# Block-quantised MLP on Trainium2: down projection as float32r products on halves, block maxima in a bank of the up projection

## The chip, the cores and the metric

The kernel runs on one core of a Trainium2 chip. The metric is device time in microseconds (us), the median of several executions. TensorE (PE) multiplies and transposes into the eight banks of PSUM; its weight loads are booked apart (PEld). VectorE (DVE) and ScalarE (ACT) read and write SBUF and the banks. GpSimd (POOL) works on SBUF here. SyncE (SP) starts the transfers.

## What is computed

Two decoder layers on `x` of 16 batches x 128 tokens x 256: attention, cross attention and an MLP each. The change is in the last MLP, which quantises every operand of its products in blocks of 32 columns:

```python
def _mx_dequant(t):
    rows, feat = t.shape
    blocks = t.reshape(rows, feat // 32, 32)
    max_abs = jnp.max(jnp.abs(blocks), axis=-1)
    scales = jnp.maximum(max_abs / 448.0, 1e-30)
    q = (blocks / scales[..., None]).astype(jnp.float8_e4m3fn).astype(jnp.float32)
    return (q * scales[..., None]).reshape(rows, feat)
...
gate = _mx_dequant(x2d) @ _mx_dequant(gate_w).T      # 256 -> 1024
up = _mx_dequant(x2d) @ _mx_dequant(up_w).T
h = jax.nn.silu(gate) * up
out = _mx_dequant(h) @ _mx_dequant(down_w).T         # 1024 -> 256
...
x = x + _L1_ffn_ref(_layernorm(x, axis=-1), L1_ffn_gate_w, L1_ffn_up_w, L1_ffn_down_w)
```

## The kernel before

The stages run one after the other, each for all 16 batches of 128 tokens. The last, `mx_mlp`, takes one batch as one tile of 128 rows. The quantised `h` of batches 0 to 13 and the quantised weights come from the stage ahead; batches 14 and 15 of `h` are quantised inside `mx_mlp` at steps 2 and 3 ("late", `scale_h` and `round_h`), and the last weights are transposed at step 1: four jobs of gate and up, and the four of down (`turn_down`), which ScalarE copies to SBUF (L2872).

A batch goes through three steps of a software pipeline; the order on each engine is written out by hand in its `step`, and semaphores count progress. The 1024 inner columns are handled as two halves `j` of 512. At step t:

- **TensorE** (`step`, L3087): for each half, gate and up products of batch t-1 (`project`, L3022, 12 products of 512 columns) and then four transposes of the quantised inner half of batch t-2 (`turn_inner`, L3032). Then two transposes of `h` of batch t (`turn_h`), then the down projection of batch t-2 (`down`, L3047): eight tiles, each a float32 product of 256 columns, which the trace shows as two passes.
- **ScalarE** (L2901): for each half `mx_silu` of batch t-1 from the gate bank, and the copy of the transposed half of batch t-2 to `innerT` (L2883). Then the high half of `hT` (L2889) and `h` of the next batch.
- **VectorE** (L2978): the sum with `x` of batch t-3 (L2968), and for each half of batch t-1 the product with up, written to the gate bank (`gate`, L2935), and `scale_inner`: block maxima (L779), scale (L773), reciprocal (L782), scaling (L783), and two steps for the rounder (L786, L788). Each waits for the one before. Between the second `gate` and its `scale_inner` stands the low half of `hT` (L2962).
- **GpSimd** (L2843): three instructions for each half, which round and multiply back (L793 to L795).

The next gate and up products of half j may start when that half has been scaled (L783). The transposes of half j wait for GpSimd and for `innerT` of the batch before to be copied. Gate and up already run as float32r products on halves: an operand is split into a high half (a copy with type float32r) and a low half (the operand minus the high half), and three products are summed: high with high, high with low, low with high (`PARTS`). In the last batch, the second half is rounded by VectorE in two pieces (`round_last_half`), and TensorE does the down projection in pieces (`last_batch`).

```python
                gate(i, j)
                if j == 1 and batch_there(t):
                    make_low(t)
                scale_inner(i, j)
```

## Time and profile before

| | |
|---|---|
| median of 3 runs | 1536.37 us (1535.61 to 1536.84) |
| the profiled execution | 1536.67 us, of it span 1534.4 us |
| TensorE busy | 1454.1 us (95%), weight loads 1206.1 us (79%) |
| VectorE busy | 1115.4 us (73%) |
| ScalarE busy | 978.9 us (64%) |
| GpSimd busy | 734.3 us (48%) |

`mx_mlp` begins at about 1353 us of the span. In the rows below, L12 is a line of the kernel. The chain of waits is followed back from what ended last: each piece shows how long the end depended on that engine. A timeline row gives start, duration, engine, line, operation, out<-in, and in brackets how long the engine was idle before it and for whom. "x12" is the number of instructions merged in a row. `bank` is any PSUM bank; `weights_even` holds the down weights in this stage. TensorE durations of a single matmul overlap with the next one: its rate is read from start to start. Granted clock of TensorE in this stage: 1.00 of 2.4 GHz.

### The profile page before, as it was taken

Reading aid. Unit: us, or ns where it says so; the run is one execution under the profiler, and the core shown is the slowest. Engines: PE = TensorE matmul, PEld = TensorE weight load, DVE = VectorE, ACT = ScalarE, POOL = GpSimd, SP = SyncE. Lnnn points to the kernel's source line nnn. Section 1 sums busy time; section 2 is a strip of 40 time slices with the busy share of each in tenths; the row PEclk is TensorE's granted clock in tenths of the full one; section 3 lists DMA queues with packets and bytes.
Section 4 is the critical chain, followed back from the end, with each engine's and each line's share of the span. In section 5 each row is a group of like instructions: output and inputs, shape, how many; then the busy total and the mean of one; then the engine's idle time right before and its main releaser. Section 6 shows DMA issues by size and latency. Waiting matters only on the chain. (4 is left out here: it accounts for less than half of the span.)

```text
span 1534.4 us, 30706 instructions
## 1 busy us (share of the span) xinstructions
PE 1454.1 (95%) x10384; PEld 1206.1 (79%) x10384; DVE 1115.4 (73%) x2539; ACT 978.9 (64%) x2620; POOL 734.3 (48%) x899
## 2 busy tenths in 40 slices
PE   5999889999999999899998999899999999989998
PEld 2666678888888888688875555489999999867887
DVE  4888668888888887554545777656777777688887
ACT  2777567777777777432325888677777787742222
POOL 3766545555555555232333433213444444457765
PEclk9999999999999999999998999999999999999999
DMA  6000020000000000000003000020000000000000
GB/s 251 2 2 2 15 87 3 5 3 3 5 3 5 4 3 1 23 1 1 1 7 132 1 2 1 9 103 8 9 8 9 8 2 2 1 1 15 14 11 18
DMA packets 15612, 29.84 MB, mean 19 GB/s; under 512 B 1506, under 2 KB 12003, under 8 KB 14691
## 3 DMA queue, kind: packets, MB, share of 16 engines
q1 hardware_dynamic: 15458, 27.89, 5.0%
q8 instruction: 85, 1.39, 0.4%
q14 instruction: 69, 0.56, 0.1%
HBM read 25.79 MB, written 2.10 MB: 18 GB/s over the span
## 5 line engine op out<-in xcount | busy, mean ns | idle before, releaser
L1468 POOL TENSOR_TENSOR weights_even<-weights_even,cross_reciprocal 128x512 f32<-128x512 f32 x64 | 66.7, 1042 | 187.4 <-DVE cross_reciprocal L1720 187.4
L945 POOL TENSOR_TENSOR cross_work<-cross_work,cross_reciprocal 128x512 f32<-128x512 f32 x64 | 66.6, 1040 | 174.8 <-DVE cross_reciprocal L1102 174.8
L1168 PE MATMUL bank<-ident,cross_work 128*128 128x128 f32 x768 | 117.3, 275 | 2.5 <-DVE cross_work L1080 2.2
L998 ACT ACTIVATE cross_work<-bank,cross_shift,cross_q_rms 128x128 f32<-128x128 f32 x256 | 113.6, 456 | 5.2 <-DVE cross_shift L1074 4.5
L1168 PEld LDWEIGHTS bank<-ident,cross_work 128*128 128x128 f32 x768 | 89.9, 141 | 30.1 <-DVE cross_work L1080 21.2
L2525 DVE TENSOR_REDUCE grouped_maxima<-bank 128x4 bf16<-128x512 f32 x128 | 82.3, 685 | 36.4 <-PE bank L2606 36.4
L2001 POOL TENSOR_TENSOR mlp_low_inner<-mlp_inner,mlp_high_inner 128x512 fp32r<-128x512 f32 x36 | 48.7, 1353 | 117.6 <-ACT mlp_high_inner L2044 117.6
L1557 ACT ACTIVATE weights_even<-bank,cross_shift 128x128 f32<-128x128 f32 x256 | 90.4, 366 | 11.1 <-DVE cross_shift L1712 10.0
L1710 DVE TENSOR_REDUCE cross_maxima<-bank 128x4 f32<-128x512 f32 x64 | 44.1, 689 | 71.8 <-PE bank L1854 71.8
L2878 ACT ACTIVATE mx_silu<-bank 128x512 f32<-128x512 f32 x32 | 19.1, 598 | 113.3 <-PE bank L3028 113.3
L404 POOL TENSOR_TENSOR causal_masked_maxima<-causal_maxima,causal_constants 128x512 bf16<-128x512 bf16 x64 | 66.5, 1060 | 46.5 <-DVE causal_maxima L552 42.1
L1193 PE MATMUL bank<-high_weights,cross_high 128*128 128x512 f32 x192 | 87.0, 453 | 0.0
L2404 ACT ACTIVATE grouped_probs<-bank 128x512 f32<-128x512 f32 x128 | 69.9, 606 | 23.5 <-PE bank L2639 23.5
L1885 PE MATMUL bank<-cross_high_wo,cross_high_heads 128*128 128x256 f32 x256 | 76.2, 298 | 8.0 <-DVE cross_low_heads L1699 7.8
L986 ACT ACTIVATE cross_high_probsT<-bank 128x512 fp32r<-128x512 f32 x64 | 38.4, 599 | 67.7 <-PE bank L1168 67.7
L2100 DVE SCALAR_TENSOR_TENSOR mlp_gated<-mlp_tanh,bank 128x512 f32<-128x512 f32 x36 | 24.7, 687 | 77.5 <-ACT mlp_tanh L2038 71.9
L1836 PE MATMUL bank<-cross_high_hT,late_high 128*128 128x256 f32 x256 | 78.0, 305 | 0.7 <-ACT weights_even L1550 0.7
L1258 PE MATMUL bank<-cross_high_wo,cross_high_heads 128*128 128x256 f32 x256 | 77.1, 301 | 0.0
L1193 PE MATMUL bank<-low_weights,cross_high 128*128 128x512 f32 x192 | 76.6, 399 | 0.0
L1193 PE MATMUL bank<-high_weights,cross_low 128*128 128x512 f32 x192 | 76.6, 399 | 0.0
L1885 PE MATMUL bank<-cross_high_wo,cross_low_heads 128*128 128x256 f32 x256 | 72.3, 282 | 0.0
L1885 PE MATMUL bank<-cross_low_wo,cross_high_heads 128*128 128x256 f32 x256 | 72.3, 282 | 0.0
(382 smaller groups left out, 5362.2 us busy)
## 6 DMA issues: line engine op xcount, KB each, us to landing
weights_even<-in_weights SPq DMA_DIRECT2D x2, 2560.0 KB, 11.6
weights_even<-in_weights SPq DMA_DIRECT2D x2, 1732.0 KB, 8.5
weights_odd_early<-in_weights SPq DMA_DIRECT2D x1, 3072.0 KB, 11.8
weights_odd_values<-in_weights SPq DMA_DIRECT2D x1, 3072.0 KB, 18.8
weights_odd_late<-in_weights SPq DMA_DIRECT2D x2, 1536.0 KB, 9.5
x<-in_x SPq DMA_DIRECT2D x4, 512.0 KB, 8.0
out<-mx_result SPq DMA_DIRECT2D x16, 128.0 KB, 1.7
weights_even<-in_weights SPq DMA_DIRECT2D x2, 512.0 KB, 5.8
```

The source lines that it names most:

```text
L404: pool.tensor_tensor(masked_maxima[g][:, :, :], maxima[s][:, g, :].unsqueeze(2).to_broadcast([P, PER, P]), later.unsqueeze(1).to_broadcast ...
L945: pool.tensor_tensor(probs[x], probs[x], reciprocal[x][:, :].unsqueeze(2).to_broadcast([P, PER, P]), ALU.mult).then_inc(probs_divided, 1)
L998: last = act.activation(probs[x][:, j, :], bank_scores[:, j * P:(j + 1) * P], ACT.Exp, scale=q_rms[x][:, j:j + 1], bias=shift[x][:, j:j + ...
L1168: last = pe.transpose(bank[:, j * P:(j + 1) * P], source, core.ident[:, :])
L1193: last = pe.matmul(out, half[:, c, :], split_weights[b][:, at:at + PER * D], start=(k == 0), stop=(k == len(jobs) - 1))
L1258: last = pe.matmul(bank_y[:, 0:EMBED], heads[x][a][:, j, :], wo_split[c][:, h, :], start=(g == 0 and m == 0), stop=(g == GROUPS - 1 and m ...
L1468: pool.tensor_tensor(probs[x], probs[x], reciprocal[x][:, :].unsqueeze(2).to_broadcast([P, JOBS, P]), ALU.mult).then_inc(probs_divided, 1)
L1557: last = act.activation(probs[x][:, j, :], bank_scores[x][:, j * P:(j + 1) * P], ACT.Exp, scale=SCALE, bias=shift[x][:, j:j + 1], accum_ou ...
L1836: last = pe.matmul(bank_q[:, j * BOTH * P:(j + 1) * BOTH * P], wqk_split[b][:, c, h * D:(h + 1) * D], hT[s][a][:, c, :, :].rearrange("p b ...
L1885: last = pe.matmul(bank_y[s][:, k * EMBED:(k + 1) * EMBED], heads[x][a][:, k * PER + j, :], wo_split[b][:, g * PER + j, :], start=(g == 0 ...
L2404: act.activation(probs[:, SLOTS * c + j, :], bank_scoresT[j][:, :], ACT.Exp, scale=SCALE)\
L2525: dve.tensor_reduce(maxima[s][:, c, 2 * pair + j, 0:PER], bank_scores[j].rearrange("p (h k) -> p h k", h=PER), AX.X, ALU.max).then_inc(max ...
```

## The change

The down projection becomes three float32r products for each tile, on halves of the inner tensor and of the down weights. ScalarE writes the high halves (`innerT[0]`, and a second copy of each piece of down weights). VectorE makes the low half of the inner tensor (`make_low_innerT`, after each `gate`), GpSimd the low half of the down weights (`low_down_weights`, two jobs after each rounding of batch 0). TensorE's `down` waits for the high half, does two products for each of four tiles, waits for the low half, does one product for each, and so for both halves. In the last batch the low halves stand behind `round_last_half` on VectorE. The block maxima of the inner halves (`largest`) are no longer in SBUF but in the first 16 columns of the up bank, which `gate` has read by then.

```diff
-    def __init__(self, layer, name, columns, places=None):
+    def __init__(self, layer, name, columns, places=None, largest=None):
         blocks = columns // BLOCK
         self.columns, self.blocks = columns, blocks
-        self.largest, self.scale, self.inverse = (layer.sbuf(f"{name}_{x}", [P, blocks])
-                                                  for x in ("largest", "scale", "inverse"))
+        self.largest = layer.sbuf(f"{name}_largest", [P, blocks]) if largest is None else largest
+        self.scale, self.inverse = (layer.sbuf(f"{name}_{x}", [P, blocks]) for x in ("scale", "inverse"))
...
-        scratch = [Scratch(layer, f"inner{j}", INTER // HALVES) for j in range(HALVES)]
+        banks_of_up = [core.banks[2], core.banks[4]]
+        scratch = [Scratch(layer, f"inner{j}", INTER // HALVES, largest=banks_of_up[j][:, 0:INTER // HALVES // BLOCK])
+                   for j in range(HALVES)]
...
-        innerT = sbuf("innerT", [P, TILES, P])
+        innerT = [sbuf(f"{half}_innerT", [P, TILES, P], F32R) for half in ("high", "low")]
+        down_split = [sbuf(f"{half}_down", [P, TILES, EMBED], F32R) for half in ("high", "low")]
...
+            def low_down_weights(jobs):
+                for k in jobs:
+                    pool.wait_ge(weights_ready, GATE_UP_JOBS - TURNED_EARLY + k + 1)
+                    tiles = slice(2 * k, 2 * k + 2)
+                    pool.tensor_tensor(down_split[1][:, tiles, :], w_down[:, tiles, :],
+                                       down_split[0][:, tiles, :].bitcast(F32), ALU.subtract).then_inc(down_low, 1)
...
+                    if isinstance(b, int) and b == 0:
+                        low_down_weights((2 * j, 2 * j + 1))
...
                         m = 2 * (k - GATE_UP_JOBS)
+                        act.activation(down_split[0][:, m:m + 2, :].rearrange("p i n -> p (i n)"),
+                                       bank_turn[k % 2][:, :], ACT.Copy)
                         act.activation(w_down[:, m:m + 2, :].rearrange("p i n -> p (i n)"), bank_turn[k % 2][:, :],
                                        ACT.Copy).then_inc(weights_ready, 1)
...
+            def copy_high_innerT(b, j):
                 act.wait_ge(innerT_filled, HALVES * b + j + 1)
                 act.wait_ge(layer.y_filled, nonneg(b))
-                act.activation(innerT[:, 4 * j:4 * j + 4, :], bank_turn[j].rearrange("p (i t) -> p i t", i=4),
-                               ACT.Copy).then_inc(innerT_ready, 1)
+                act.activation(innerT[0][:, 4 * j:4 * j + 4, :], bank_turn[j].rearrange("p (i t) -> p i t", i=4),
+                               ACT.Copy).then_inc(innerT_high, 1)
...
+            def make_low_innerT(b, j):
+                dve.wait_ge(innerT_high, HALVES * b + j + 1)
+                dve.tensor_tensor(innerT[1][:, 4 * j:4 * j + 4, :], bank_turn[j].rearrange("p (i t) -> p i t", i=4),
+                                  innerT[0][:, 4 * j:4 * j + 4, :].bitcast(F32), ALU.subtract).then_inc(innerT_low, 1)
...
                         if j == 1 and batch_there(t):
                             make_low(t)
+                        if batch_there(t - 2):
+                            make_low_innerT(t - 2, j)
                         scale_inner(i, j)
...
+                if t - 2 == VERY_LAST:
+                    make_low_innerT(VERY_LAST, 0)
+                    for k in range(PIECES):
+                        make_low_last_piece(k)
...
-                pe.wait_ge(innerT_ready, nonneg(HALVES * (b - 1) + j + 1))
+                pe.wait_ge(innerT_low, nonneg(HALVES * (b - 1) + j + 1))
...
+            def down_products(tiles, parts, first=False, last=False):
+                jobs = [(m, a, b) for m in tiles for a, b in parts]
+                for k, (m, a, b) in enumerate(jobs):
+                    product = pe.matmul(bank_y[:, 0:EMBED], innerT[a][:, m, :], down_split[b][:, m, :],
+                                        start=(first and k == 0), stop=(last and k == len(jobs) - 1))
+                return product
+
+            WITH_HIGH, WITH_LOW = ((0, 0), (0, 1)), ((1, 0),)
+
             def down(b):
                 pe.wait_ge(result_ready, nonneg(b))
-                for m in range(TILES):
-                    if m % 4 == 0:
-                        pe.wait_ge(innerT_ready, HALVES * b + m // 4 + 1)
-                    last = pe.matmul(bank_y[:, 0:EMBED], innerT[:, m, :], w_down[:, m, :],
-                                     start=(m == 0), stop=(m == TILES - 1))
-                last.then_inc(layer.y_filled, 1)
-
-            def down_tiles(tiles):
-                for m in tiles:
-                    last = pe.matmul(bank_y[:, 0:EMBED], innerT[:, m, :], w_down[:, m, :],
-                                     start=(m == 0), stop=(m == TILES - 1))
-                return last
+                for j in range(HALVES):
+                    tiles = range(4 * j, 4 * j + 4)
+                    pe.wait_ge(innerT_high, HALVES * b + j + 1)
+                    down_products(tiles, WITH_HIGH, first=(j == 0))
+                    pe.wait_ge(innerT_low, HALVES * b + j + 1)
+                    product = down_products(tiles, WITH_LOW, last=(j == HALVES - 1))
+                product.then_inc(layer.y_filled, 1)
...
-                pe.wait_ge(innerT_ready, HALVES * VERY_LAST + 1)
-                down_tiles(range(half // 2))
+                pe.wait_ge(innerT_high, HALVES * VERY_LAST + 1)
+                down_products(range(half), WITH_HIGH, first=True)
                 turn_piece(0)
-                down_tiles(range(half // 2, half))
+                pe.wait_ge(innerT_low, HALVES * VERY_LAST + 1)
+                down_products(range(half), WITH_LOW)
                 turn_piece(1)
                 for k in range(PIECES):
-                    pe.wait_ge(last_copied, k + 1)
-                    last = down_tiles(tiles_of(k))
-                last.then_inc(layer.y_filled, 1)
+                    pe.wait_ge(last_high, k + 1)
+                    down_products(tiles_of(k), WITH_HIGH)
+                    pe.wait_ge(last_low, k + 1)
+                    product = down_products(tiles_of(k), WITH_LOW, last=(k == PIECES - 1))
+                product.then_inc(layer.y_filled, 1)
...
-                        pe.wait_ge(weights_ready, WEIGHT_JOBS - TURNED_EARLY)
+                        pe.wait_ge(down_low, WEIGHT_JOBS - GATE_UP_JOBS)
```

VectorE in the steady part, from the second gate product of a batch; before (`mx_low_hT` is the low half of `hT`):

```order
L2935 TENSOR_TENSOR bank<-mx_silu,bank 128x512
L2962 TENSOR_TENSOR mx_low_hT<-bank,mx_high_hT 128x256
L779 TENSOR_REDUCE mx_inner_largest<-bank 128x16
L773 SCALAR_TENSOR_TENSOR mx_inner_scale<-mx_inner_largest,least_scale 128x16
L782 RECIPROCAL mx_inner_inverse<-mx_inner_scale 128x16
L783 TENSOR_TENSOR mx_inner_scaled<-bank,mx_inner_inverse 128x512
L786 TENSOR_SCALAR mx_inner_rounder<-mx_inner_scaled 128x512
L788 TENSOR_SCALAR mx_inner_rounder<-mx_inner_rounder 128x512
L2968 TENSOR_TENSOR mx_result<-bank,x 128x256
```

and after, at the same place on VectorE:

```order
L2950 TENSOR_TENSOR bank<-mx_silu,bank 128x512
L2977 TENSOR_TENSOR mx_low_hT<-bank,mx_high_hT 128x256
L2982 TENSOR_TENSOR mx_low_innerT<-bank,mx_high_innerT 128x512
L779 TENSOR_REDUCE bank<-bank 128x16
L773 SCALAR_TENSOR_TENSOR mx_inner_scale<-bank,least_scale 128x16
L782 RECIPROCAL mx_inner_inverse<-mx_inner_scale 128x16
L783 TENSOR_TENSOR mx_inner_scaled<-bank,mx_inner_inverse 128x512
L786 TENSOR_SCALAR mx_inner_rounder<-mx_inner_scaled 128x512
L788 TENSOR_SCALAR mx_inner_rounder<-mx_inner_rounder 128x512
L2995 TENSOR_TENSOR mx_result<-bank,x 128x256
```

One instruction of 128x512 comes in ahead of the reduction, and the maxima go through a bank; the same holds for the first half, without `mx_low_hT`. GpSimd at the first batches of the stage, the difference (`mx_low_down` is the low half of the down weights; the last two rows belong to the late `h`):

```order
 L795 TENSOR_TENSOR mx_inner_q<-mx_inner_scaled,mx_inner_scale 128x512
-L793 TENSOR_TENSOR mx_inner_scaled<-mx_inner_scaled,mx_inner_rounder 128x512
-L794 TENSOR_TENSOR mx_inner_scaled<-mx_inner_scaled,mx_inner_rounder 128x512
-L795 TENSOR_TENSOR mx_inner_q<-mx_inner_scaled,mx_inner_scale 128x512
+L2842 TENSOR_TENSOR mx_low_down<-weights_even,mx_high_down 128x512 x2
+L793 TENSOR_TENSOR mx_inner_scaled<-mx_inner_scaled,mx_inner_rounder 128x512
+L794 TENSOR_TENSOR mx_inner_scaled<-mx_inner_scaled,mx_inner_rounder 128x512
+L795 TENSOR_TENSOR mx_inner_q<-mx_inner_scaled,mx_inner_scale 128x512
+L2842 TENSOR_TENSOR mx_low_down<-weights_even,mx_high_down 128x512 x2
 L793 TENSOR_TENSOR mx_h_scaled<-mx_h_scaled,mx_h_rounder 128x256
 L794 TENSOR_TENSOR mx_h_scaled<-mx_h_scaled,mx_h_rounder 128x256
```

Two instructions stand ahead of the rounding of the second half of batch 0, and two ahead of the first late `h`.

## Rows read from the trace of the kernel before

**Rows 1.** Chain of waits, 1440 to 1485 us: start us, us, what (TensorE, one batch).
```profile
1450.12 3.46 PE bank L3052 x16
1453.58 2.80 PE bank L3028 x12
1456.38 0.44 PE bank L3036 x4
1456.82 2.79 PE bank L3028 x12
1459.61 0.44 PE bank L3036 x4
1460.05 0.22 PE bank L3044 x2
```

**Rows 2.** The same chain, a batch in which it goes through VectorE and GpSimd.
```profile
1473.29 1.11 DVE mx_inner_scale L773
...
1476.41 1.29 POOL mx_inner_scaled L793
...
1479.14 1.06 POOL mx_inner_q L795
...
1480.25 0.66 PE bank L3036 x4
```

**Rows 3.** Timeline of ScalarE: start us, us, instruction; `mx_silu` of batches 3 and 15.
```profile
1396.75 0.60 ACT L2878 ACTIVATE mx_silu<-bank 128x512 f32<-128x512 f32 x1 [2.15 <-PE bank L3028]
...
1521.25 0.60 ACT L2878 ACTIVATE mx_silu<-bank 128x512 f32<-128x512 f32 x1 [2.15 <-PE bank L3028]
```

**Rows 4.** Timeline of GpSimd, the instruction under way when L773 of [rows 2] began.
```profile
1473.08 1.27 POOL L794 TENSOR_TENSOR mx_inner_scaled<-mx_inner_scaled,mx_inner_rounder 128x512 f32<-128x512 f32 x1
```

**Rows 5.** L773 and L786, 1400 to 1510 us: durations ns min/median/max, starts, shape.
```profile
L773 DVE SCALAR_TENSOR_TENSOR mx_inner_scale<-mx_inner_largest,least_scale x22: 174/930/1106, 1400.7 to 1509.8; 128x16 f32<-128x16 f32 x22
...
L786 DVE TENSOR_SCALAR mx_inner_rounder<-mx_inner_scaled x21: 426/427/429, 1402.6 to 1506.0; 128x512 int32<-128x512 int32 x21
```

**Rows 6.** Groups by line, 1340 to 1540 us: busy us, mean ns, idle before.
```profile
L783 DVE TENSOR_TENSOR mx_inner_scaled<-bank,mx_inner_inverse 128x512 f32<-128x512 f32 x32 | 22.1, 691 | 1.1
...
L779 DVE TENSOR_REDUCE mx_inner_largest<-bank 128x16 f32<-128x512 f32 x32 | 21.9, 686 | 0.6
...
L782 DVE RECIPROCAL mx_inner_inverse<-mx_inner_scale 128x16 f32<-128x16 f32 x32 | 8.1, 253 | 1.1
L2962 DVE TENSOR_TENSOR mx_low_hT<-bank,mx_high_hT 128x256 fp32r<-128x256 f32 x16 | 6.8, 424 | 3.0 <-ACT mx_high_hT L2889 2.6
...
L2975 DVE TENSOR_TENSOR late_low<-bank,late_high 128x512 fp32r<-128x512 f32 x4 | 2.5, 684 | 0.4 <-ACT late_high L2868 0.4
```

**Rows 7.** Timeline, VectorE and GpSimd, last batch: an L788 that meets GpSimd.
```profile
1525.05 1.11 POOL L795 TENSOR_TENSOR mx_inner_q<-mx_inner_scaled,mx_inner_scale 128x512 f32<-128x512 f32 x1
1525.28 1.15 DVE L788 TENSOR_SCALAR mx_inner_rounder<-mx_inner_rounder 128x512 f32<-128x512 f32 x1
```

**Rows 8.** Timeline of TensorE, cross attention: float32r products of 256 columns.
```profile
1300.16 0.28 PE L1885 MATMUL bank<-cross_high_wo,cross_high_heads 128*128 128x256 f32 x1
...
1301.48 0.28 PE L1885 MATMUL bank<-cross_high_wo,cross_low_heads 128*128 128x256 f32 x1
```

**Rows 9.** Timeline, first batches: ScalarE copies of down weights; down(0), products of batch 2.
```profile
1363.21 1.09 ACT L2872 ACTIVATE weights_even<-bank 128x512 f32<-128x512 f32 x2 [0.25 <-PE bank L3018]
...
1373.28 3.62 PE L3052 MATMUL bank<-weights_even,mx_innerT 128*128 128x256 f32 x16
...
1377.69 0.50 PE L3028 MATMUL bank<-late_high,mx_high_hT 128*128 128x512 f32 x1 [0.79 <-DVE mx_low_hT L2962]
```

**Rows 10.** GpSimd, L2001 in an earlier stage: durations ns min/median/max, starts, shape.
```profile
L2001 POOL TENSOR_TENSOR mlp_low_inner<-mlp_inner,mlp_high_inner x36: 1260/1292/1899, 643.8 to 799.1; 128x512 fp32r<-128x512 f32 x36
```

**Rows 11.** Timeline of VectorE, end: last rounding and last sum.
```profile
1528.85 0.42 DVE L2954 TENSOR_TENSOR mx_inner_q<-mx_inner_scaled,mx_inner_scale 128x256 f32<-128x256 f32 x1
...
1531.81 0.42 DVE L2968 TENSOR_TENSOR mx_result<-bank,x 128x256 f32<-128x256 f32 x1 [2.54 <-PE bank L3058]
```

More of the change, by code:

```diff
@@ L2894, in copy_last_piece @@
                 first = TILES // HALVES + TILES_A_PIECE * k
[L2895 removed]
+                act.activation(innerT[0][:, first:first + TILES_A_PIECE, :],
                                last_banks[k][:, 0:PIECE].rearrange("p (i t) -> p i t", t=P),
[L2897 removed]
+                               ACT.Copy).then_inc(last_high, 1)
             fetch_h(0)
```

18 lines of the change are left out of this document (11 added, 7 removed).

## The prediction

> **What bounds the kernel now.** Only the last stage is touched, so I read only that: the 181 us from 1353 us on. I begin with the chain of waits over a steady batch [rows 1]. TensorE stands in it without a gap: the down projection 3.46 us, a half of gate and up 2.80 us, four transposes 0.44, the other half 2.79, four transposes 0.44, and the two transposes of the next `h` 0.22. That is 10.15 us of TensorE for a batch. The starts of `mx_silu` for the second halves [rows 3] give the measured period: from batch 3 to batch 15, 124.50 us for 12 batches, 10.38 each. So TensorE is the limit, but not alone. In about one batch of four the chain leaves it and comes back through VectorE and GpSimd [rows 2]: GpSimd's rounding of the second half ends at 1480.20 and the transposes start at 1480.25, later than TensorE alone would have had them. This second path is nearly as long as the first, and the change shortens the first one.
>
> What makes the second path long is one tiny operation. The block scale, L773, works on 16 columns and takes 0.17 us at best, 0.93 at the median and 1.11 at most [rows 5]. The instance at 1473.29 lasted 1.11 us and ended at 1474.40; GpSimd's instruction that began at 1473.08 and took 1.27 ended at 1474.35 [rows 2, 4]. It was waiting for GpSimd. Operations with one operand in a bank do not do this: L783 has a mean of 691 ns, and L2962 one of 424 [rows 6]. The third kind is the `tensor_scalar` from SBUF to SBUF (L786, L788), 0.43 us undisturbed [rows 5]. It does wait: the one at 1525.28 took 1.15 us and ended at 1526.43, 0.27 after GpSimd's instruction of 1525.05 [rows 7].
>
> **Down projection (TensorE).** 16 passes of 256 columns in 3.46 us [rows 1] become 24 products in float32r. The same form stands in the cross attention: L1885, 256 columns, starts at 1300.16 and, eleven products later, at 1301.48 [rows 8], so 0.12 us each. 24 x 0.12 = 2.88 us, and TensorE's loop falls from 10.16 to 9.58. I take 0.12, because it has the same types, sizes and a weight load for each product. The Trainium skill, "TensorE: Matmul & The Clock Gate", section "Back-to-back issue gap", has N/2.4 + 2.5 ns between matmuls, 109 ns here. The estimate by that page is 2.62 us a batch and about 1.8 us less in the whole sum; the row at 0.12 decides against it.
>
> **Low half of the inner tensor (VectorE).** Two subtractions of 128x512 a batch. The nearest row is L2975, 684 ns, bank and SBUF in, float32r out [rows 6]. I take 0.68, less 0.09 because independent instructions overlap by that much. What is queued behind each is the reduction of the next half, then the rounding, GpSimd, and TensorE's transposes.
>
> **Block maxima in a bank (VectorE).** L773 then has one operand in SBUF. No row shows this form. Its bounds are 0.17 us, the shortest L773 [rows 5], which I take, and 0.25, the reciprocal of the same 16 columns [rows 6]; L773 as now, waiting for GpSimd, is a rival. L779 writes the bank and reads one, as L2935 does; I leave its 0.69. The Trainium skill, "SBUF — State Buffer", section "Who interferes with whom", says that a VectorE instruction with at most one SBUF input, outside the two-port modes, does not contend with GpSimd. No run here shows it for this form yet.
>
> **The new period.** Take T as the moment when TensorE finishes the second half of gate and up of batch b.
> - First half, VectorE: its `mx_silu` ends at T-2.43. Then gate product 0.03+0.69, low half 0.60, reduction 0.61, scale 0.21, reciprocal 0.29, scaling 0.73, L786 and L788 0.47 each: T+1.64. (0.03 of every chained step is the gap behind it; 0.09 off every independent one is the overlap.)
> - GpSimd rounds this half from T+1.78, 1.28+1.28+1.05 and two gaps of 0.08, to T+5.55 (lengths as in [rows 2]; the middle one is as long as the first).
> - Second half, VectorE: gate product to 2.24, low `hT` to 2.58, low half to 3.17, reduction 3.78, scale 3.98, reciprocal 4.27, scaling 4.99. L786 would start at 5.03, meets GpSimd's third instruction and is over at 5.55+0.27 = 5.82; L788 at 6.28. GpSimd: 6.42 to 10.19. TensorE can start these transposes at T+10.25.
> TensorE by itself would be there at T+9.58. A late start of the transposes pushes the next T by the same amount, so period P and lateness d obey P = 9.58+d and d = 10.25-P: P = 9.91. **Of the 0.58 us taken from TensorE, 0.33 is lost again to the wait for GpSimd.** From batch 3 to 15: 12 x 9.91 = 118.9 against 124.5, **-5.6 us**.
>
> **The start of the stage.** Three things are added there.
> - ScalarE copies each piece of the down weights twice. Now a pair of copies takes 1.09 us, with 0.25 idle before the second pair [rows 9]. Four more at 0.49 are 1.96, some 0.3 of which fills what was idle: the next high `hT` and the products of batch 1 are +1.6.
> - GpSimd makes four low halves of the weights. Row of the same form: L2001, 1.26 to 1.90 us, median 1.29 [rows 10]. Two stand ahead of the rounding of (0, 1) and two ahead of the late `h`, whose quantisation on VectorE works from SBUF to SBUF and waits behind each. Gate product (1, 0) comes 2.5 late (1.6 of it from above) and gate product (1, 1) 3.1. TensorE's down(0), now at 1373.28, waits for the fourth low half until about 1376.8, hidden by what follows: its last four products wait for the low inner half on VectorE, until 1381.3. The products that start at 1377.69 [rows 9] then start about 4.1 us later.
> - Batches 1 to 3 are bound by VectorE with the late `h` in it: two low halves, +1.2, against 0.9 from L773: +0.3.
> Together **+4.4 us** at batch 3. With low halves of 1.5 us instead of 1.29 it would be 0.6 more, at 1.9 us 2 more.
>
> **The end.** For the last batch the low half of tiles 0 to 3 stands on VectorE behind the six roundings, the last of which begins at 1528.85 [rows 11]. TensorE waits for it, then has 24 short products in pieces instead of 16. I lay that out as **+1.4 us** between the last `mx_silu` and the last sum at 1531.81 [rows 11].
>
> **Sum.** +4.4 - 5.6 + 1.4 = +0.2. The same way of laying out, applied to the kernel before, gives 10.33 a batch where the rows have 10.38, 0.5 us too little over the twelve; I expect it to omit the same of the new one: +0.7. The profiled execution took 1536.67 us (span 1534.4), 0.3 above the median of 1536.37. Median plus 0.7: **1537.1 us**, which nobody could tell from no change; a measurement of this kernel tells about 0.2% (3.1 us) apart.
>
> **Rivals.**
> - *TensorE alone sets the period* (faster). The path over GpSimd would have to be 0.67 shorter than I have it, by L786 not meeting GpSimd (0.36) and shorter gaps. Then P = 9.58, 12 x 0.33 = 4.0 less: 1533.1. Against it speak [rows 7] and that the two paths already alternate [rows 2].
> - *TensorE waits for the low half* (slower). In my layout the low inner half of the second half is ready at T+3.24 and wanted at T+0.33+0.66+2.40 = 3.39, a margin of only 0.15. If VectorE comes later by more than that, each further 0.1 is 0.1 a batch, and the gain is gone while the start and the end stay. L786 of a first half meeting GpSimd's last instruction would do it; it starts at T+0.74 and GpSimd is done at about T+0.28. With 0.5 late: 12 x 0.35 = +4.2, 1541.3. For it: the small margin; against it: 0.46 us of distance to the collision.
> - *The bank does not free L773 from GpSimd* (slower, the change does not do what it says). Then both halves have a scale of 0.6 to 1.1 and the low half on top. The period becomes about 10.5: 12 x 0.6 = 7.1, and 1.3 more in start and end: 1545.5. Against it are L783 and L2962 [rows 6].
>
> **How the numbers follow.** My forecast 0.62, first rival 0.16, second 0.14, third 0.06, something else 0.02. The low end is the first rival's 1533.1, which is also about the bound for faster. The high end is the second's 1541.3, and takes in low weight halves of 1.9 us. Outside are the third rival and the tails, about 0.15. Faster by over 0.2% 0.17, within 0.62, slower 0.21.
>
> **What would show it.** After: L773 at 0.17 to 0.25 us for the inner halves without exceptions; products of the down projection every 0.12 us; second-half `mx_silu` starts 9.9 apart, with TensorE waiting about 0.3 us a batch for GpSimd's L795; some L786 of 0.7 to 0.8 us; `mx_silu` of batch 3 about 4.4 us later than now, that of batch 15 about 1.2 earlier. I am wrong if the period is 9.6 or 10.2, if waits for the low inner half appear in the steady part, or if the start costs under 3 or over 6 us.

## The result, and the profile after

The changed kernel takes 1542.59 us, the median of 5 runs (1540.48 to 1543.31); the kernel before took 1536.37 beside it (1534.73 to 1540.06). The ratio is 1.0036, with a 95% interval of 1.0023 to 1.0049: it is slower, by 6.2 us. The prediction was 1537.1, nothing that could be told from no change, with a high end of 1541.3. It was wrong: slower, and outside its range.

The profiled execution has a span of 1539.8 us, against 1534.4. To see where the time went I measure three parts of the last stage in the profile of each kernel: the **start**, from the first copy of `h` to the `mx_silu` of the second half of batch 3; the **steady** part, from there to the same instruction of batch 15; and the **end**, from there to the start of the last sum with `x`.

| part, us | before | after | difference | predicted |
|---|---|---|---|---|
| start | 43.58 | 49.33 | +5.75 | +4.4 |
| steady, 12 batches | 124.50 | 121.21 | -3.29 | -5.6, with the shortfall -5.1 |
| end | 10.56 | 13.97 | +3.41 | +1.4 |
| sum | 178.64 | 184.51 | +5.87 | +0.7 |

Every part was 1.4 to 2.0 us worse than predicted. Below, "the stage" is the sum of the three parts. One thing about the steady part has to be known to read it. In the kernel before, the first of its twelve intervals, from batch 3 to batch 4, takes 11.62 us and the other eleven 10.26 on average; in the kernel after all twelve take 10.10 or 10.11. So 1.51 of the 3.29 us gained lie in that one interval. The stage of the kernel after starts at 1352.67. The rows that end its three parts are these, timeline of ScalarE and then of VectorE; they answer to [rows 3, 11]:

```profile
1402.00 0.60 ACT L2893 ACTIVATE mx_silu<-bank 128x512 f32<-128x512 f32 x1 [2.15 <-PE bank L3061]
...
1523.21 0.60 ACT L2893 ACTIVATE mx_silu<-bank 128x512 f32<-128x512 f32 x1 [2.15 <-PE bank L3061]
```

```profile
1537.18 0.42 DVE L2995 TENSOR_TENSOR mx_result<-bank,x 128x256 f32<-128x256 f32 x1 [1.72 <-PE bank L3083]
```

**The slow clock.** The view to read for the start and the end is the busy time by stretch. Its columns are the stretch, its length, the busy time of TensorE, its weight loads, VectorE, ScalarE and GpSimd, the granted clock of TensorE (1.00 is 2.4 GHz, 0.50 is 1.2 GHz), and DMA. Kernel after:

```profile
1352.00:1367.00 15.00, 11.24 (x63) 8.98 (x64) 9.77 (x25) 10.50 (x21) 5.18 (x5) 1.00 0.01 2
1367.00:1371.00 4.00, 4.00 (x13) 3.10 (x13) 3.77 (x7) 0.12 (x1) 3.10 (x4) 0.59 0.00 0
...
1394.00:1399.00 5.00, 5.00 (x21) 4.01 (x20) 2.72 (x7) 0.24 (x1) 4.02 (x4) 0.66 0.07 26
1399.00:1403.00 4.00, 4.00 (x25) 3.41 (x24) 3.44 (x7) 1.85 (x5) 1.32 (x2) 1.00 0.00 0
1523.00:1530.50 7.50, 4.77 (x35) 4.14 (x35) 7.16 (x15) 1.79 (x3) 3.84 (x4) 1.00 0.00 1
1530.50:1534.00 3.50, 2.81 (x15) 2.40 (x14) 2.61 (x7) 0.38 (x1) 0.00 (x0) 0.53 0.11 37
```

From 1367 to 1371 TensorE is busy all the time and gets through 13 instructions, at a clock of 0.59. The same length of time at 1.00, from 1399 to 1403, holds 25, though several of those are short transposes; the fairer comparison is that of twelve equal products below. There are four such stretches (the one not shown is around 1383, at 0.74); the kernel before shows 1.00 in the same places up to the end of its work. Each of them follows a wait. The timeline of TensorE shows one and what came behind it; the bracket is the idle time before the row, the first column the start:

```profile
1393.63 0.80 PE L3083 MATMUL bank<-mx_high_down,mx_low_innerT 128*128 128x256 f32 x4 [1.75 <-DVE mx_low_innerT L2982]
1394.23 0.63 PE L3061 MATMUL bank<-late_high,mx_high_hT 128*128 128x512 f32 x1
1394.66 0.63 PE L3061 MATMUL bank<-late_low,mx_high_hT 128*128 128x512 f32 x1
...
1397.86 0.40 PE L3061 MATMUL bank<-late_high,mx_high_hT 128*128 128x512 f32 x1
1398.09 0.40 PE L3061 MATMUL bank<-late_low,mx_high_hT 128*128 128x512 f32 x1
```

After 1.75 us of waiting for the low inner half, products of 512 columns start 0.43 us apart, and later 0.23 again. The twelve products and what is between take from 1394.23 to 1398.56, 4.33 us, where the chain before had 2.79 to 2.80 for the same twelve [rows 1]. VectorE then has to wait for `mx_silu`, so this stretch is on the path:

```profile
1399.39 0.70 DVE L2950 TENSOR_TENSOR bank<-mx_silu,bank 128x512 f32<-128x512 f32 x1 [2.50 <-ACT mx_silu L2893]
```

At the end it is the wait for GpSimd, before the transposes of the last batch, and a second one right behind it:

```profile
1528.75 0.66 PE L3069 MATMUL bank<-ident,mx_inner_q 128*128 128x128 f32 x4 [1.85 <-POOL mx_inner_q L795]
...
1530.18 0.36 PE L3083 MATMUL bank<-mx_high_down,mx_high_innerT 128*128 128x256 f32 x1 [0.78 <-ACT mx_high_innerT L2898]
```

**The steady part.** The chain of waits now returns through VectorE and GpSimd in every batch; once round it takes two batches (start us, us, what):

```profile
1471.68 1.06 POOL mx_inner_q L795
...
1472.78 0.66 PE bank L3069 x4
1473.44 0.22 PE bank L3077 x2
1473.66 3.07 PE bank L3083 x24
1476.73 2.82 PE bank L3061 x12
...
1480.20 0.71 DVE bank L2950
...
1480.93 0.69 DVE mx_low_innerT L2982
...
1484.37 0.62 DVE bank L2950
...
1487.90 0.69 DVE mx_inner_rounder L786
...
1491.85 1.06 POOL mx_inner_q L795
```

From the end of one rounding at 1472.74 to the end of that two batches on, at 1492.91, are 20.17 us; the `mx_silu` starts of all twelve batches are 10.10 us apart. The part of the change that concerns single instructions did as announced. Groups of the kernel after, from its lines and its groups by shape (durations in ns: min/median/max, or busy us and mean), which answer to [rows 5, 6, 10]:

```profile
L773 DVE SCALAR_TENSOR_TENSOR mx_inner_scale<-bank,least_scale x32: 174/174/175, 1360.1 to 1526.7; 128x16 f32<-128x16 f32 x32
```

```profile
L2982 DVE TENSOR_TENSOR mx_low_innerT<-bank,mx_high_innerT 128x512 fp32r<-128x512 f32 x31 | 21.3, 686 | 0.6
L786 DVE TENSOR_SCALAR mx_inner_rounder<-mx_inner_scaled 128x512 int32<-128x512 int32 x32 | 18.3, 572 | 1.1
...
L2842 POOL TENSOR_TENSOR mx_low_down<-weights_even,mx_high_down 128x512 fp32r<-128x512 f32 x4 | 5.1, 1304 | 0.0
```

### The profile page after: what moved, and what is told of

It is laid out like the page before. It is cut to its first block and busy times, and to the rows that moved or that the text cites. A ratio compares the mean times of both kernels' runs of the same rounds, so it can differ in the third digit from the quotient of the medians.

```text
span 1539.8 us, 31003 instructions
## 1 busy us (share of the span) xinstructions
PE 1456.0 (95%) x10512; PEld 1210.5 (79%) x10512; DVE 1122.5 (73%) x2572; ACT 982.2 (64%) x2624; POOL 740.8 (48%) x903
## 3 DMA queue, kind: packets, MB, share of 16 engines
q8 instruction: 86, 1.41, 0.4%
## 5 line engine op out<-in xcount | busy, mean ns | idle before, releaser
L2001 POOL TENSOR_TENSOR mlp_low_inner<-mlp_inner,mlp_high_inner 128x512 fp32r<-128x512 f32 x36 | 48.8, 1355 | 117.3 <-ACT mlp_high_inner L2044 117.3
```

## The experiments

Two theories had to be told apart. **Theory A**: the misses of the start and the end are the slow clock after TensorE's waits, and the miss of the steady part is something else, VectorE's wait for its own gate product. **Rival**: the layout of the start and the end is simply too short (GpSimd's and VectorE's work there was under-priced), and the clock hides in time that nobody waits for. All stage figures are from one profile each; two profiles of the kernel after (after, e13_again) differ by 0.05 us in the stage. The medians stand beside them, each with its ratio to runs of the kernel before that were measured with it (medians 1536.3 to 1537.5), since single runs of the whole program scatter by several us. What each kernel is stands in its section below.

| kernel | start | steady | end | stage | median | ratio (95%) |
|---|---|---|---|---|---|---|
| before | 43.58 | 124.50 | 10.56 | 178.64 | 1536.37 | |
| after | 49.33 | 121.21 | 13.97 | 184.51 | 1542.59 | 1.0036 (1.0023 to 1.0049) |
| e13_again | 49.30 | 121.19 | 13.97 | 184.46 | 1541.52 | 1.0038 (1.0024 to 1.0053) |
| e1_fill | 47.85 | 121.20 | 12.17 | 181.22 | 1537.66 | 1.0009 (0.9990 to 1.0028) |
| e2_late_wait | 47.48 | 119.20 | 12.04 | 178.72 | 1536.34 | 0.9999 (0.9982 to 1.0016) |
| e8_late_and_fill | 47.59 | 119.25 | 12.06 | 178.90 | 1537.46 | 1.0002 (0.9985 to 1.0020) |
| e5_vector_low | 47.13 | 121.20 | 12.56 | 180.89 | 1540.06 | 1.0016 (0.9997 to 1.0035) |
| e10_late_vector | 46.25 | 119.15 | 13.50 | 178.90 | 1537.53 | 0.9997 (0.9980 to 1.0014) |
| e4_split_only | 50.07 | 126.65 | 14.54 | 191.26 | 1548.01 | 1.0070 (1.0056 to 1.0084) |
| e3_maxima_only | 42.57 | 123.15 | 10.58 | 176.30 | 1535.09 | 0.9991 (0.9979 to 1.0002) |
| e9_maxima_late | 42.44 | 122.71 | 10.57 | 175.72 | 1534.11 | 0.9984 (0.9964 to 1.0004) |
| e11_split_inside | 43.41 | 121.33 | 12.55 | 177.29 | 1534.63 | 0.9982 (0.9968 to 0.9996) |
| e12_split_inside_b | 42.43 | 121.52 | 12.70 | 176.65 | 1533.27 | 0.9978 (0.9969 to 0.9987) |
| e14_split_4_to_13 | 42.47 | 121.59 | 10.57 | 174.63 | 1532.44 | 0.9973 (0.9962 to 0.9984) |

### Filling TensorE's waits

The same kernel, with products into an unused place where TensorE waits in batches 0 to 2 and in the last one:

```diff
+            def fill(place, columns, count, first=True):
+                for k in range(count):
+                    pe.matmul(place, w_gate[0][:, 0, 0:P], w_gate[0][:, 0, 0:columns], start=first, stop=first)
...
             def project(b, j):
+                if isinstance(b, int) and b == 1 and j == 0:
+                    fill(bank_y[:, :], 512, 7)
...
                     down_products(tiles, WITH_HIGH, first=(j == 0))
+                    if isinstance(b, int) and b < 2 and j == 1:
+                        fill(bank_y[:, EMBED:2 * EMBED], EMBED, 14, first=False)
...
+                pe.wait_ge(scale_chain, SCALE_STEPS * HALVES * VERY_LAST + 4)
+                fill(bank_up[0][:, :], 512, 8)
                 turn_inner(VERY_LAST, s, 0)
+                fill(bank_up[0][:, :], 512, 3)
                 pe.wait_ge(result_ready, VERY_LAST)
...
                 turn_piece(0)
+                fill(bank_up[0][:, :], 512, 5)
                 pe.wait_ge(innerT_low, HALVES * VERY_LAST + 1)
```

> The changed kernel, with products that nobody reads put into TensorE's long waits: 7 of 512 columns ahead of the products of batch 1, 14 of 256 columns into the unused half of the y bank ahead of the low products of the second half in down(0) and down(1), 8, 3 and 5 of 512 columns around the transposes of the last batch. Theory 1 (TensorE's clock fell to the lower level after those waits; that cost 1.4 us at batch 3 and 1.9 us at the end): granted clock 1.00 throughout, batch 3 products 2.9 us instead of 4.3, total 3.3 us less than the changed kernel, about 1539.3. Theory 2 (the time went into the waits themselves and the clock is a side effect, hidden by VectorE): the same 1542.6, or a little more from the extra products.

The granted clock of the same stretches in e1_fill:

```profile
1367.00:1371.00 4.00, 4.00 (x21) 3.23 (x20) 3.80 (x7) 1.09 (x2) 3.10 (x4) 1.00 0.00 0
...
1394.00:1399.00 5.00, 5.00 (x27) 4.14 (x26) 3.86 (x9) 1.09 (x2) 4.02 (x4) 1.00 0.07 26
...
1530.50:1534.00 3.50, 3.16 (x22) 2.49 (x20) 1.77 (x5) 0.42 (x2) 0.00 (x0) 1.00 0.00 0
```

More work for TensorE, and the stage is 3.29 us shorter: start 1.48, end 1.80, steady unchanged at 10.10 a batch. So the slow clock cost 3.3 us, and only in two of its four stretches. The chains of the start show which. Kernel after, and then e1_fill:

```profile
1392.97 0.61 DVE mx_low_innerT L2982
...
1394.43 4.31 PE bank L3061 x12
```

```profile
1393.05 0.61 DVE mx_low_innerT L2982
...
1394.44 2.82 PE bank L3067 x12
```

Up to VectorE's low half of batch 1 nothing is gained, although the first two slow stretches are gone; the whole 1.49 us are in the twelve products of batch 3 behind it. The first two are hidden behind VectorE. e2_late_wait below agrees: it keeps them and has nearly the same start as e8_late_and_fill (47.48 and 47.59), which doesn't.

### The changed kernel once more

> The changed kernel once more, unchanged, to see whether the slow stretches of TensorE belong to the kernel or to one execution. Theory (they follow its waits of 1.75 us and more, which are in the program): granted clock under 0.9 again in the four stretches behind the waits for the low inner halves and for GpSimd (0.5 to 0.8 there), stage 184.0 to 185.0, median 1541 to 1543.5. Rival (chance of one execution): clock 1.00 throughout and a stage of 181.2, like the kernel with filled waits.

The stage is 184.46 us, the clock 0.66, 0.74, 0.66 and 0.54 in the four stretches (1366 to 1371, 1379 to 1385.5, 1394 to 1399, 1530.5 to 1537). The slow clock belongs to this program and not to one execution.

### VectorE's wait for its own gate product

```diff
             def gate(i, j):
                 dve.wait_ge(silu_ready, i + 1)
                 dve.tensor_tensor(bank_gate[j][:, :], silu[j][:, :], bank_up[j][:, :], ALU.mult)\
                    .then_inc(inner_ready, 1)
-                dve.wait_ge(inner_ready, i + 1)
 
             def scale_inner(i, j):
+                dve.wait_ge(inner_ready, i + 1)
```

> The changed kernel, with VectorE's wait for its own gate product moved from behind the product to ahead of the reduction that reads it. Theory 1 (the low half of the inner tensor stands right behind that wait, so it starts 0.12 us later than it could, once a half, which lengthens the path to GpSimd and makes TensorE wait): second-half mx_silu starts 9.95 apart instead of 10.10, 1.1 to 2 us less in all, about 1541. Theory 2 (the period is held by something else, such as TensorE's products themselves): 10.10 and 1542.6 as before.

The chain of e2_late_wait, to be held against the one of the kernel after:

```profile
1478.28 0.53 DVE bank L2950
...
1478.89 0.68 DVE mx_low_innerT L2982
...
1485.71 0.84 DVE mx_inner_rounder L786
...
1491.81 2.87 PE bank L3083 x24
```

The low half starts 0.61 us behind the gate product instead of 0.73. Both halves of a batch gain that 0.12, and TensorE's down projection takes 2.87 us instead of 3.07, since it no longer stops for the low half. L786 gives 0.15 back, because it meets GpSimd's last instruction for longer. The period is 9.93. In the whole stage this one line brings 5.79 us: 2.01 steady, 1.85 at the start and 1.93 at the end. The expectation had the period right and the sum too small, 1.1 to 2 us for all. The part that it lacked, start and end, comes mostly from the clock, which stayed at 1.00 in batch 3 and at the end. That is why filling adds nothing to it, with both edits in one kernel:

> Both together: VectorE's wait for its own gate product is put ahead of its reader (as in e2_late_wait) and products into an unused place of a bank fill TensorE's waits at the start and at the end (as in e1_fill). Their results are read by nobody. Theory (the late wait already kept the clock up at batch 3 and at the end, so that filling finds little left): batch 3 at 47 to 47.6 us, period 9.93, end 12.0, stage 178 to 179, the same as with the late wait alone (178.7). Rival (the two gains are independent, -5.8 and -3.3): stage 175.4.

178.90 us, the theory's number. The gains of e1_fill and e2_late_wait are largely the same gain.

### Half of the change at a time

e3_maxima_only is the kernel before with `largest` in the up bank (the first lines of the change alone); e4_split_only is the changed kernel with `largest` back in SBUF:

```diff
-        scratch = [Scratch(layer, f"inner{j}", INTER // HALVES, largest=banks_of_up[j][:, 0:INTER // HALVES // BLOCK])
-                   for j in range(HALVES)]
+        scratch = [Scratch(layer, f"inner{j}", INTER // HALVES) for j in range(HALVES)]
```

> The kernel before, with only the block maxima moved to the up bank; the down projection stays float32. Theory 1 (the scale no longer waits for GpSimd, so the batches in which the path over GpSimd was late lose that, and VectorE is faster in batches 1 to 3): 10.28 or less a batch instead of 10.38, batch 3 about 1 us earlier, together 2 us less than before, about 1534.4. Theory 2 (TensorE bounds the stage, so a faster scale is worth nothing): 1536.4.

> The changed kernel, with the block maxima back in SBUF; the down projection in halves. Theory 1 (each scale waits for GpSimd again, 0.6 to 1.1 us, on the path that now sets the period): 10.5 a batch, 5 to 7 us above the changed kernel, about 1548. Theory 2 (the maxima in the bank matter little, the float32r products carry the change): 1542.6 within 1 us.

The maxima alone make the stage 2.34 us shorter, the split alone 12.62 us longer. With both the stage is 5.87 longer, so the split costs 8.2 us on top of the maxima. In e4 L773 waits for GpSimd again (174 to 856 ns, median 538), and the chain shows where a long L773 leads when the split stands behind it:

```profile
1453.08 0.69 DVE mx_inner_scale L773
...
1456.76 0.61 DVE mx_low_innerT L2981
1457.37 0.04 issue
1457.41 0.74 PE bank L3082 x4
1458.15 2.82 PE bank L3060 x12
```

This is the second rival of the prediction, TensorE waiting for the low half, and it appears with the third: the twelve intervals average 10.55, and from batch 4 on each is 10.6. In e3 the chain is TensorE without a gap, 10.15 us a batch from batch 4 on. What [rows 2] showed, the excursion over GpSimd in one batch of four, is gone.

The late wait, the same edit as in e2_late_wait, in the kernel e3_maxima_only:

> The kernel before with the block maxima in the bank (as in e3_maxima_only) and with VectorE's wait for its own gate product put ahead of its reader; the down projection is float32, unsplit. Theory (there TensorE's own loop of 10.15 us is the period, and VectorE's wait cannot shorten it): period 10.15 in the steady part against 10.26, the gain being only the first interval; start and end 0.1 to 0.3 shorter; stage 175.0 to 176.3. Rival (the wait costs there what it cost in the changed kernel, 0.17 a batch): period 10.0 to 10.1, stage 174.0. If the theory holds this is as fast as the changed kernel can be made with its longer start and end, so that splitting the down projection gives nothing.

The period stays 10.15, the stage is 175.72, as the theory said: there TensorE has no use for 0.12 us on VectorE.

### The low down weights on VectorE

```diff
+            def low_down_weights():
+                for k in range(WEIGHT_JOBS - GATE_UP_JOBS):
+                    dve.wait_ge(weights_ready, GATE_UP_JOBS - TURNED_EARLY + k + 1)
+                    m = 2 * k
+                    dve.tensor_tensor(down_split[1][:, m:m + 2, :].rearrange("p i n -> p (i n)"), bank_turn[k % 2][:, :],
+                                      down_split[0][:, m:m + 2, :].rearrange("p i n -> p (i n)").bitcast(F32),
+                                      ALU.subtract).then_inc(down_low, 1)
...
                         gate(i, j)
+                        if isinstance(t, int) and t == 1 and j == 1:
+                            low_down_weights()
...
-                    if isinstance(b, int) and b == 0:
-                        low_down_weights((2 * j, 2 * j + 1))
...
-                        act.activation(w_down[:, m:m + 2, :].rearrange("p i n -> p (i n)"), bank_turn[k % 2][:, :],
-                                       ACT.Copy).then_inc(weights_ready, 1)
```

e5_vector_low has this edit alone, e10_late_vector the late wait as well.

> The changed kernel, but the low halves of the down weights are made by VectorE out of the bank (4 subtractions of 128x512, after the second half of gate and up of the second batch) instead of by GpSimd: ScalarE copies each piece once, and GpSimd's four instructions of 1.3 us at 1366.08 and 1373.23 are gone. Theory (what costs at the start is ScalarE's second copies, GpSimd's four instructions, and the slow clock that follows TensorE's waits for them): the late h and the rounding come earlier, TensorE's longest wait before batch 3 is under 1.5 us and its clock stays up in more of the stretch; second-half mx_silu of batch 3 at 46.0 to 47.5 us after the stage's start (49.3 in the changed kernel, 43.6 before), stage 181 to 183 us instead of 184.5. Rival (VectorE is the bound of the start, so its own 4 x 0.68 = 2.7 us are added): batch 3 at 50 to 52, stage 185 to 187. The steady period stays 10.10.

> The changed kernel with both the late wait and the low halves of the down weights made by VectorE. Theory: the gains add where they are in different places: batch 3 at 44.5 to 45.7 us (47.5 with the late wait alone), period 9.93, end 12.0; stage 176 to 177, level with the kernel before with the maxima in the bank. Rival (VectorE is the bound of the start): batch 3 at 48.5 to 50, stage 180 to 181.

e5 gave a start of 47.13 and a stage of 180.89, against 50 to 52 and 185 or more for the rival: VectorE's own length was not added to the start. One sign of the theory did not come: TensorE's longest wait before batch 3 was 2.71 us and not under 1.5. (The `mx_silu` of batch 1 came later than in the kernel after, at 22.54 instead of 21.44: the pieces of weights in the banks now wait 1.90 us for VectorE, and the clock was at 0.50 behind that wait, from 1368 to 1374. It was made up in batch 2.) The end is 1.41 us shorter than in the kernel after, with the same program and nearly the same waits (1.84 and 0.78 us); the clock was back at 1.00 from about 1535, before the last twelve products, and in the kernel after it was not. So the price of a slow stretch also hangs on how long it lasts. e10 missed its expectation by 2 us: 46.25 at batch 3, and an end of 13.50 instead of 12.0, with the clock at 0.50 again. That end has the same program as e2's, and nearly the same wait before it. Timeline of TensorE, e2_late_wait and then e10_late_vector:

```profile
1526.03 0.65 PE L3069 MATMUL bank<-ident,mx_inner_q 128*128 128x128 f32 x4 [1.71 <-POOL mx_inner_q L795]
```

```profile
1380.22 0.74 PE L3082 MATMUL bank<-mx_high_down,mx_low_innerT 128*128 128x256 f32 x4 [2.59 <-DVE mx_low_innerT L2971]
...
1524.61 0.66 PE L3068 MATMUL bank<-ident,mx_inner_q 128*128 128x128 f32 x4 [1.70 <-POOL mx_inner_q L795]
```

and the granted clock behind them, again e2 and then e10:

```profile
1527.40:1531.00 3.60, 2.20 (x17) 1.99 (x17) 2.97 (x7) 0.38 (x1) 0.00 (x0) 1.00 0.10 36
```

```profile
1380.20:1384.00 3.80, 3.78 (x21) 3.20 (x21) 3.59 (x9) 0.21 (x1) 2.90 (x3) 1.00 0.00 0
...
1526.00:1529.50 3.50, 3.18 (x13) 2.81 (x14) 3.06 (x7) 0.38 (x1) 0.00 (x0) 0.50 0.11 37
```

1.71 us of waiting and the clock stays, 1.70 and it falls, 2.59 and it stays. The length of the last wait does not decide it alone, and no run here says what else does.

### Splitting only where it pays

The start and the end are bound by VectorE and by latency, not by TensorE; only the steady part can use a faster product. So batches 0 to 2 (e11) or 0 to 3 (e12) and batch 15 go back to float32 products, which need no low halves, and the low down weights are made later. Both have the bank maxima and the late wait.

```diff
+        def whole(b):
+            return b < 4 or (True and b == VERY_LAST)
...
+            def whole_products(tiles):
+                for m in tiles:
+                    last = pe.matmul(bank_y[:, 0:EMBED], innerT_whole[:, m, :], w_down[:, m, :],
+                                     start=(m == 0), stop=(m == TILES - 1))
+                return last
...
-                        if batch_there(t - 2):
+                        if batch_there(t - 2) and not whole(t - 2):
                             make_low_innerT(t - 2, j)
```

> The split only where TensorE is the bound: batches 0 to 2 and batch 15 are projected down in float32 as before, batches 3 to 14 as float32r products on halves. The high halves of the down weights are copied by ScalarE from SBUF in steps 2 and 3, the low halves are made by GpSimd one at a time after each rounding of batches 1 and 2. Block maxima in the bank, VectorE's wait for its own gate product ahead of its reader. Theory: start near the unsplit kernel (batch 3 at 42.4), plus what four more GpSimd instructions of 1.3 us cost VectorE, 0.5 each: 43.5 to 45; period 9.93; end 10.6; stage 173.5 to 175, the median 3 to 5 us under the kernel before. Rival (the four low halves on GpSimd cost their full length, 5.2 us): batch 3 at 47.5, stage 177.5.

> The same with batches 0 to 3 in float32 and the four low halves of the down weights made one step later, after the roundings of (2, 1), (3, 0) and (3, 1, two of them), where no late h is quantised any more. Theory: one more batch at 10.15 instead of 9.93, and GpSimd's extra instructions fall on steps in which GpSimd has more idle time: batch 3 to 15 within 120.5, batch 3 at 42.5 to 43.5, stage 173 to 174.5. Rival (after batch 3 the path over GpSimd sets the time, so each extra instruction costs its length): stage 177 to 178.

The start came out as short as without the split in e12 (42.43, against 42.44 in e9) and 1 us longer in e11 (43.41). The end did not: 12.55 and 12.70 instead of 10.6, with the very products of the kernel before. So both stages missed their range, 177.29 and 176.65 against at most 175 and 174.5. (177.29 is near the number of e11's rival, but that one had batch 3 at 47.5.) The clock had fallen again, behind a wait that is longer because the down projection before it is shorter. Hence the last run, in which batch 14 is not split either:

```diff
-            return b < 4 or (True and b == VERY_LAST)
+            return b < 4 or b >= VERY_LAST - 1
```

> As e12_split_inside_b, but batch 14 too is projected down in float32, so that only batches 4 to 13 are split. In e12_split_inside_b TensorE stood still for 1.68 us before the transposes of the last batch (1521.19) and then ran at 0.50 to 0.57 of its clock from 1523 to 1526; the end took 12.7 us instead of 10.6. Theory (the slow clock there comes from that wait, and a down projection that is 0.5 us longer shortens the wait to about 1.1 us, as in the kernel with whole products): clock 1.00 to the end, end 10.5 to 10.8, stage 174.3 to 175.0, median 1531 to 1533. Rival (the end is longer for another reason, such as the low halves still in VectorE's row): end 12 to 12.7, stage 176.5.

The wait before the transposes of the last batch, e12 and then e14:

```profile
1521.19 0.66 PE L3080 MATMUL bank<-ident,mx_inner_q 128*128 128x128 f32 x4 [1.68 <-POOL mx_inner_q L795]
```

```profile
1521.11 0.66 PE L3080 MATMUL bank<-ident,mx_inner_q 128*128 128x128 f32 x4 [0.68 <-POOL mx_inner_q L795]
```

and the stretch that follows, in the same order:

```profile
1523.00:1526.00 3.00, 3.00 (x10) 2.31 (x9) 1.61 (x4) 0.38 (x1) 0.00 (x0) 0.52 0.12 44
```

```profile
1523.00:1526.00 3.00, 3.00 (x18) 2.59 (x17) 1.11 (x3) 0.77 (x2) 0.00 (x0) 1.00 0.00 0
```

The wait became 1.0 us shorter: TensorE comes 0.6 later (3.46 us of products instead of 2.87), and GpSimd's result, 5.42 us behind the last `mx_silu` in e12, is there after 4.96, since VectorE has no low half of batch 14 to make. So of the 2.1 us between the two ends 0.46 is the rival's, VectorE's row. The other 1.67 lie behind the start of those transposes, where both kernels have the same instructions and the clock is the difference that the profiles show. The end is 10.57, the stage 174.63, 4.0 us shorter than before. The median of 1532.44 stands against 1537.53 of the kernel before measured beside it, a ratio of 0.9973 (0.9962 to 0.9984). This version beats both kernels. Of its 4.0 us, 2.9 are the maxima and the late wait (e9), about 1.1 the split. The 1.1 is read from the two profiles; the medians of e9 and e14, with overlapping intervals, don't tell the two kernels apart.

e12's other expectation, a steady part of at most 120.5, was missed by 1.0: with GpSimd making low weights, the interval from batch 4 to 5 was 10.98 to 11.00 us, and L786 and L788 waited for it.

## Why the prediction was wrong, point by point

- **The start, +5.75 against +4.4.** With the clock held up (e1) it is +4.27. So the terms for ScalarE's copies, GpSimd's four instructions (1.30 us each, 1.29 taken) and VectorE were right in sum. What failed is a step that isn't there: I laid out new waits of TensorE in batches 0 to 2 and let it go on at the rate it had before, with 2.80 us for twelve products, where behind the wait of 1.75 us in down(1) they took 4.33. The prediction itself had the last four products of down(0) wait until 1381.3 (measured 1380.51, in a stage that starts 0.50 earlier), some 2 us by its own figures and 1.97 in the trace. So such waits were known and their consequence was not asked for. Cost: 1.48 us.
- **The steady part, -3.3 against -5.1.** I took 0.09 off for two independent instructions on VectorE everywhere. Behind the gate product there is none: the code waits there for its own product before going on, whatever comes next, and the low half ends 0.71 us behind it where I had 0.60. The low half stands right behind it, and the second one was ready too late for TensorE: the margin of 0.15 that the second rival named was used up, with small stops of TensorE inside the down projection (3.07 us against 2.88). e2 gives the whole of it: period 9.93 where I had 9.91, steady part -5.3. The mechanism and the formula were right; the term that failed is the step from the gate product to what follows, 0.12 too small, twice a batch.
- **The yardstick for the steady part.** I read 10.38 us a batch as the period of the kernel before. It is the mean of one interval of 11.62 and eleven of 10.26. My layout of 10.33 was thus 0.07 too long for a steady batch and not 0.05 too short, and the correction of 0.5 us had no ground. It did little harm, since the prediction took 12 x 9.91 from the whole 124.50. But the period itself falls by 0.16 from before to after, and by 0.22 from e9 (10.15) to e2 (9.93), which is what the split gives a batch.
- **The end, +3.41 against +1.4.** With the clock held up it is +1.61. The same step failed as at the start: TensorE's products behind a wait of 1.85 us were taken at the rate they had before. The slow clock cost 1.80 us.
- **The sum.** 1.48 + 1.80 for the clock and 2.01 for the late wait in the steady part are 5.3 us, and the stage missed its +0.7 by 5.2. What is left of each part is within about 0.2 us. The slow clock is shown by e1, the gate product's wait by e2. Neither was among the rivals by itself: the second rival had the right place and sign for the steady part and was priced for it at up to 4.2, but it left the start and the end alone.
- **What was right.** L773 at 174 ns in all 32 instances: the bank frees it from GpSimd. The Trainium skill, "SBUF — State Buffer", section "Who interferes with whom", which the prediction quoted, holds here, and the third rival came near its numbers (period 10.5, 1545.5 us) when the bank was taken away (10.55 and 1548.0). Products stood 0.12 us apart. The formula quoted beside them, of the Trainium skill, "TensorE: Matmul & The Clock Gate", section "Back-to-back issue gap", is given there for a single product by itself and not for a stream of products with weight loads; nothing in the sum rests on it. VectorE's low half took 0.69 us. L786 took 0.69 where it meets GpSimd in the steady part (0.7 to 0.8 foreseen) and 0.43 elsewhere there.
- **The chances.** 0.21 went to slower over 0.2%, which is what came. All three parts missed by 1.4 to 2.0 us on the same side. One case does not show it, but a likely reason is that a layout with fixed durations leaves waits out more easily than it puts one too many in.

## What to carry to other kernels

When a change makes TensorE faster where it isn't the only bound, it turns part of its work into waiting. Look at what it waits for in the sparse stretches (the first and last batches of a pipeline), and price what follows the new waits once more with the clock at 1.2 GHz, as the bad case: here it came behind some of them and not behind others. A split pays only where the engine it relieves is the bound: here in ten batches of sixteen, and not in the one ahead of a long wait.

Before pricing work that is put between two instructions, look at whether the first is followed by a wait for itself. Moving such a wait down to its reader was worth 5.8 us in the split kernel, 2.0 of them by itself and most of the rest because the clock stayed up, and 0.6 in the unsplit one, where that path was not the bound.

## What the runs showed of the hardware

- **The clock fell in a stage in which TensorE never stood still for long.** In the kernel after, the granted clock dropped from 1.00 toward 0.50 behind waits of 1.89, 1.97, 1.75 and 1.85 us, and in its second profile behind the same waits within 0.02 us. It did not behind waits of 0.68 and 1.11 us at the end of e14 and e9 (with 0.78 more behind the transposes), nor in the kernel before with 1.63 at the start of the stage and 1.09 to 1.29 later. The Trainium skill, "TensorE: Matmul & The Clock Gate", section "Why this matters for your kernels", warns of gaps between bursts of products that are longer than any in this stage; these runs show the fall with shorter ones. What exactly sets it off stays open: 1.70 us led to it in e10, 1.71 did not in e2, 1.77 did not in e11, 2.59 did not in e10, and 2.71 did not in e5. Products in the waits (e1, e8) kept the clock at 1.00 up to the last sum.
- **A faster product can be slower for this reason.** In e12 the down projection ahead of the last batch is 0.6 us shorter than in e14, and the end is 2.1 us longer, 1.67 of it behind the wait, where the clock is 0.52 and not 1.00. The product is not all of the difference: 0.46 us of the longer wait come from VectorE's low half of batch 14.
- **A wait between independent instructions costs VectorE 0.12 us** (start to start 0.73 against 0.61 for 128x512 with a bank operand). The Trainium skill, "VectorE: DVE Perf Modes", section "The DRAIN you can't avoid", has a chain of copies in which the semaphore costs nothing extra; here, between VectorE's product and its subtraction, it did, and the measurement decides.
